# Layer two of a graph network: GpSimd's gather waits for VectorE's additions instead of TensorE's sums

## The reference, cut to what matters

```python
messages = relu(concatenate([x[src], x[dst]]) @ W_msg + b_msg)     # 200000 x 256
aggregated = segment_sum(messages, dst, 12500)
h = relu(concatenate([x, aggregated]) @ W_upd + b_upd)
y = (h - mean(h)) * rsqrt(var(h) + 1e-5) * gamma + beta
out = layernorm(x + y)
```

## Time and profile before

| what | us |
|---|---|
| median of three runs (lowest, highest) | 4386.48 (4386.21, 4386.79) |
| span of the profiled execution | 4403.8 |
| TensorE matmuls busy in it | 3810.6 (87%) |
| VectorE busy | 3380.9 (77%) |
| ScalarE busy | 2779.1 (63%) |
| GpSimd busy | 2477.9 (56%) |
| gathers of layer two, line 795, x1612 | 1543.0 busy, 890.8 idle before them |

### The profile page before, as it was taken

How to read it: one execution, slowest core, us unless ns; L and a number is a source line. 1 busy time by engine, 2 the same in 40 slices (tenths; PEclk the granted TensorE clock), 3 DMA queues, 4 the chain that set the end, 5 groups by cost and what they waited for, 6 DMA issues and landing times.

```text
span 4403.8 us, 85804 instructions
## 1 busy us (share of the span) xinstructions
PE 3810.6 (87%) x26341; PEld 3176.6 (72%) x26341; DVE 3380.9 (77%) x7638; ACT 2779.1 (63%) x7247; POOL 2477.9 (56%) x2585
## 2 busy tenths in 40 slices
PE   4999999899999999956888888878888888888886
PEld 4999999788888888845666666666666666666665
DVE  7999999799999999955666666666666666666666
ACT  4888888777777777744555555555555555555554
POOL 2653655344455555536666666666666666666662
PEclk8999999999999999988899999999999989999998
DMA  5776544567777777743444444444444444444442
GB/s 133 243 231 226 190 189 188 197 191 206 209 209 209 209 209 208 206 141 110 127 142 129 136 127 140 132 130 136 131 132 136 135 131 131 128 129 139 131 131 72
DMA packets 344434, 707.82 MB, mean 161 GB/s; under 512 B 58153, under 2 KB 201334, under 8 KB 343954
## 3 DMA queue, kind: packets, MB, share of 16 engines
q0 software_dynamic: 114912, 359.18, 29.2%
q1 hardware_dynamic: 229074, 343.13, 23.1%
HBM read 507.96 MB, written 195.74 MB: 160 GB/s over the span
## 4 chain that ended last, share of the span: by engine, by line
PE 44%; DVE 29%; issue 11%; another core or an unknown queue 9%; ACT 2%; DVEq 2%; DMA 2%; SPq 1%; POOL 0%; ACTq 0%; POOLq 0%
PE ps L1327 11%; PE ps L1339 10%; DVE big L1903 7%; PE ps L1157 6%; DVE scr L1753 4%; PE ps L1305 4%; DVE arena L1913 3%; DVE arena L1756 3%; PE ps L1219 2%; PE ps L1164 2%; PE ps L1230 2%; PE ps L1188 2%; DVE scr L1756 1%; PE ps L1147 1%
## 5 line engine op out<-in xcount | busy, mean ns | idle before, releaser
L795 POOL DMA_INDIRECT arena<-d_p,tabs x1612 | 1543.0, 957 | 890.8 <-issue 457.3
L1913 DVE TENSOR_TENSOR arena<-arena,ps 128x512 f32<-128x512 f32 x806 | 527.0, 683 | 760.9 <-remote 503.8
L1327 PE MATMUL ps<-arena 128*128 128x256 f32 x3224 | 897.3, 419 | 240.1 <-DVE big L1903 174.2
L1111 ACT ACTIVATE arena<-arena 128x1024 f32<-128x1024 f32 x403 | 425.7, 1056 | 1004.8 <-DVE arena L1913 956.3
L1339 PE MATMUL ps<-big,scr 128*128 x3224 | 840.3, 401 | 219.6 <-DVE arena L1913 134.4
L1327 PEld LDWEIGHTS ps<-arena 128*128 128x128 f32 x3224 | 627.7, 205 | 424.2 <-ACT arena L1111 192.3
L1339 PEld LDWEIGHTS ps<-big,scr 128*128 128x128 f32 x3224 | 641.9, 202 | 356.9 <-issue 261.1
L1903 DVE SCALAR_TENSOR_TENSOR big<-big,tabs,ps 128x256 f32 x1612 | 767.8, 476 | 105.7 <-DVE big L1903 47.7
L781 POOL DMA_INDIRECT arena<-d_m,scr x392 | 531.2, 1355 | 564.0 <-DVE arena L1756 220.8
L1305 PE MATMUL ps<-arena,scr 128*128 128x256 f32 x2620 | 614.9, 384 | 10.5 <-DVE arena L1756 10.3
L1305 PEld LDWEIGHTS ps<-arena,scr 128*128 128x128 f32 x2620 | 483.7, 190 | 93.2 <-issue 32.9
(11 more groups left out here) (285 smaller groups left out, 5753.3 us busy)
## 6 DMA issues: line engine op xcount, KB each, us to landing
d_m<-arena SPq DMA_DIRECT2D x108, 603.0 KB
arena<-d_loc SPq DMA_DIRECT2D x135, 384.0 KB
d_m<-arena SPq DMA_DIRECT2D x108, 402.0 KB
arena<-d_p,tabs POOLq DMA_INDIRECT x1612
arena<-in_xT_dram SPq DMA_DIRECT2D x96, 256.0 KB
d_xp<-arena SPq DMA_DIRECT2D x49, 256.0 KB, 3.3
arena<-d_xp SPq DMA_DIRECT2D x49, 256.0 KB
d_x<-arena SPq DMA_DIRECT2D x49, 256.0 KB
```

Of the source, the lines that this page charges most:

```text
L795: e.indirect_dma_start(out=G1[j % 8][:, k, :], out_offset=None, in_=d_p, in_offset=bass.IndirectOffsetOnAxis(ap=tabS[:, j, k:k + 1], axis= ...
L1111: e.activation(G1[g % 8], G1[g % 8], ACT.Relu).then_inc(S("f_re"), 1)
L1327: m = e.matmul(turn(H, AB)[:, k * 256:k * 256 + 256], OH1[(j - 2) % 4][:, 2 * h + k, :], G1[(j - 2) % 8][:, 2 * h + k, :], start=True, sto ...
L1913: e.tensor_tensor(v, v, q2(turn(2 * j + h, QB)[:, :]), ALU.add).then_inc(S("f_m"), 1)
```

## The change

The wait in front of a group's four gathers is on another semaphore. Before, GpSimd waits until `f_ag` shows 2 (j - 7), which is that TensorE's sums of group j-8 are done. After, it waits until `f_acc` shows 4 (j - 7), which is that VectorE's four additions of group j-8 are done. In both, the first eight groups wait for nothing.

```diff
             def gath(j, g, i):
-                waitn(e, "f_ag", 2 * (j - 7))
+                waitn(e, "f_acc", 4 * (j - 7))
                 for k in range(4):
                     e.indirect_dma_start(out=G1[j % 8][:, k, :], out_offset=None, in_=d_p,
                                          in_offset=bass.IndirectOffsetOnAxis(ap=tabS[:, j, k:k + 1], axis=0)).then_inc(S(f"f_g{j % 8}"), 16)
```

## The result

The kernel with the change takes 4768.74 us (median of four runs, 4766.91 to 4772.59), the kernel before 4386.64 us beside it (four runs, 4386.21 to 4404.7). The ratio is 1.0865, with a 95% interval from 1.0845 to 1.0886: 8.7% slower, some 382 us. Three of the four runs before lie at 4386 to 4387 us and one at 4404.7, near the span of the profiled execution, 4403.8; against that one alone the change is 8.3% slower. The forecast was 4918 us with its own range from 4740 to 5230.

A forecast was written before the change was run, and what follows sets the result against it. Layer two was taken to be bound by cycles of GpSimd's gather runs plus late TensorE signals; (7.3 - 5.95) x 394 groups = 532 us on 4386.5 gave 4918 us, own range 4740 to 5230, or 4376 to 5230 including no change.

The forecast's parts named there:

- That it costs, and why: Layer two: GpSimd starts later in each cycle, 7.3 us a group instead of 5.95, 532 us more; slower given 0.67.
- the release: Layer two: the moment TensorE's held signals arrive, put 2.88 us after the end of a three-group run of gathers.
- "f_qe", TensorE's signal, is what VectorE lacks: VectorE's wait before line 1913: the unnamed "remote" sender, 467.2 us in 133 waits, is TensorE's queries, not the gather.
- The landing of the rows, 0 us: Layer-two gathers: shifted 4 to 11 us later, they keep over 15 of 30 us lead, so cost nothing.
- Three groups a cycle: Changed layer two: three groups per run of gathers, 21.9 us a cycle, 7.3 a group; two or four as ends.
- The steps' agreement with the kernel before: The same cycle steps gave the old kernel two groups in 11.8 us, 5.9 a group, against 5.95 measured.
- 4.3 + 2.88 us of idle time a cycle: GpSimd in layer two: 4.3 us waiting for VectorE's additions after the release, 2.88 from run's end to release.
- the 17.3 us: Whole kernel: the profiled span, 4403.8 us, lies 17.3 above the median run of 4386.48, a gap the forecast kept.
- What would show it: Signs: idle before line 795 some 1300 us, some 130 waits of 7 us, VectorE stalls 8 to 10 us.
- No change (4386): Rival: TensorE's lateness is its own, so the new wait only delays gathers that are 30 us early; chance 0.20.
- Faster (4012): Rival: signals are held because GpSimd waits on TensorE's count; moving it saves 374 us; chance 0.13 for faster.
- the hold: Layer two: TensorE signals posted over some 3 to 7 us into a gather run arrive 2 to 3 us after it.

The follow-up runs named there:

- f1_sums_next: Kernel before, but GpSimd waits for TensorE's sums of group j-7 instead of j-8, on a chip where signals come late: 4402.04 against 4404.76 us, ratio 0.9995.
- e6_half_gathers: Kernel before with two of each group's four gathers left out, the message waiting for two landings: 3746.44 against 4403.32 us, ratio 0.8509.
- f3_sync_loads: Kernel before with SyncE loading the row buffers by direct DMAs of consecutive rows instead of GpSimd's gathers: 3741.66 against 4404.76 us, ratio 0.8493.

## Why the prediction was right, and where its sizes were off

**That it costs, and why.** As predicted. GpSimd's start moved from the release to behind the additions; f1_sums_next shows that the lost lead alone costs nothing, and e6_half_gathers and f3_sync_loads that the wait for "remote" goes when the back-to-back gathers by GpSimd go. That it was measured on a holding chip at all, like the trace that the forecast was read from, was luck; the forecast didn't know of the other kind.

**"f_qe", TensorE's signal, is what VectorE lacks.** Right, by the semaphore changes above; the kernel after shows it too: at 2729.46 and 2730.82 the halves are taken one by one, and of VectorE's two counts only `f_qe` goes by halves, while both are recorded done by 2721.56.

**The landing of the rows, 0 us.** Held: no wait of line 1913 is put down to a gather in the kernel after.

**Three groups a cycle.** Mostly. Counted over all starts of the gather line in the kernel after, 144 runs follow the first: 107 of three groups, 34 of two, two of one and one of four, 2.74 on average. Of the query halves recorded less than 5 us into a run for which VectorE stood ready, 113 passed within 1 us and 2 didn't; between 5 and 7 us it is 40 and 67, beyond 7 us 6 and 138. So the edge isn't sharp, and now and then a cycle is cut to two. The steps' agreement with the kernel before, for which they were trusted, was partly luck: its 225 stops of over 0.6 us lie behind 91 runs of one group, 99 of two and 35 of three, and signals under 5 us old were held there 56 times in 157. That all three kinds cost about the same, 6.1, 5.85 and 5.85 us a group, is why 5.9 came out. (The tail's four messages in 18.15 us are 4.54 us each and not 4.53; nothing hangs on it.)

**4.3 + 2.88 us of idle time a cycle.** This is the term that was mis-sized. Measured, GpSimd stands 5.4 us a cycle (768.5 / 142), 6.07 in the median after a run of three and 2.82 after one of two, where the sum had 7.18. The part that failed is the release, 2.88 us after the run. In the 107 cycles of three the last release of VectorE before GpSimd starts comes on average 2.0 us after the run's end, and from it to GpSimd's start it is 4.1 us, so the 4.3 for the additions was nearly right. Counted from the first release instead, it is 0.25 and 5.8 us, because the two halves often come apart (2729.46 and 2730.82); in 20 of the 107 that first release lies over 2 us ahead of the run's end. Cycles of three are 14.7 + 6.1 = 20.8 us, 6.9 a group; those of two 9.7 + 3.2 = 12.9, 6.4 (means). Together 6.9, as measured. With 6.87 for 7.3 my sum would give 0.92 x 394 = 363 us and 4749; measured 4768.74. Most of the rest is the 17.3 us by which I let a run lie below its profile: the change's median lies 2.2 us below its own profiled span (4770.9), and 4403.8 + 363 = 4767 is near both.

**What would show it.** The idle time before line 795 rose to 1267.3 ("some 1300"), the waits are 142 ("some 130") and of 5.4 us ("7 us"). VectorE's stalls average 5.7 and reach 10.1 us ("8 to 10"). The sentence that GpSimd's idle time begins 2 to 3 us before VectorE's stall ends holds roughly for the last release (2.0 us) and not for the first, as above. Of its signs of being wrong, queries that pass at ages above 7 us did occur, 6 of 144.

**The rivals.** No change (4386) fits what free chips show for the neighbours of the change, but for another reason than mine: not that the lateness is TensorE's own, but that there is none there. Faster (4012) fell: GpSimd no longer waits on TensorE's count and the signals are held all the same; e6_half_gathers has the old wait and none is held. Its price was well read, however: a kernel whose GpSimd never waits takes 4034 to 4038 us. The rule of the Trainium skill (SBUF — State Buffer, section "SBUF: two separate sides") that TensorE waits for nobody gave 4386; it agrees with the free chips' traces, where TensorE works beside 18.1 us of gathers in 24, and on holding chips, where the first stall is 29.15 us before and 21.29 us after, the measurement decides against reading it as "GpSimd can't delay TensorE's work": the reads may wait for nobody, and still the signals come late.

Not settled: what holds the signals, and why some chips do it. It is shown that on such a chip the hold is there with back-to-back indirect gathers by GpSimd and gone with half of them or with SyncE's loads in their place. Whether a GpSimd that is merely busy does it too, and whether plain transfers from its queue would, was not tried there.

## What to carry to other kernels

A wait that is met long before it is needed can still set the time, if a stretch of the program runs in cycles: ask at which point of the cycle the waiting engine starts, not how much lead it has. When three engines stand and one works, and the wait's sender has no name, look whether signals come long after the work that posts them; the working engine is then a suspect: thin it out by half or do its job from another queue, and see whether the wait goes. Compare times within one chip only, and look in each trace whether the thing to be tested is there before reading a null result as an answer.

## What was not expected of the hardware

- One kernel, 4386 to 4405 us in three sets of runs (chips 8 and 11, and the first, whose number isn't on record) and 4034 to 4038 us in two (chips 7 and 15). The effect accounts for it: layer two starts at 1946 to 1950 us in both kinds, and 5.95 - 5.08 = 0.87 us a group over 403 groups is 351 us.
- TensorE's signals come late in a line, in their order, 0.06 us apart once it moves, while recorded signals of VectorE and ScalarE in the same trace are on time.
- Taking the back-to-back gathers off GpSimd brings the ratio to 0.849 with the same number of bytes moved (of other rows). Part of that is the hold (5.95 us a group where a free chip has 5.08), the rest is that without GpSimd's issue rate the period falls to TensorE's 4.35.
- Behind a hold comes a slow restart: the two matmuls of half a group take 2.07 us instead of 1.03, and the granted clock over layer two fell from 0.92 to 0.85.
